# The first block of x in two transfers of 4 KB pieces, four neighbouring tokens to a partition

## Chip, cores and metric
One core of one Trainium2 chip runs the whole program. The metric is the device time of the program in microseconds (us).

## What is computed
All data are fp32; x has 2048 tokens of 512 features. Each token is normalised, goes through an attention over its own 32 heads (no token looks at another) and through a gated feed-forward layer, and the two results are multiplied and added to x. Nothing couples two tokens, so the tokens may be dealt out to partitions in any order, if the result is put back in the same order.

```python
xn = (x - mean(x)) / sqrt(var(x) + 1e-5)                       # per token
q = xn @ Wq + bq; k = repeat(xn @ Wk + bk, 4); v = repeat(xn @ Wv + bv, 4)
scores = einsum('bsdh,bseh->bsde', q, k) / 4                   # 16 x 16 per token
s = einsum('bsde,bseh->bsdh', softmax(scores), v)
nx = xn * rsqrt(mean(xn**2) + 1e-5) * ln_w
f = (silu(nx @ gate_w.T) * (nx @ up_w.T)) @ down_w.T           # 512 -> 1792 -> 512
out = x + s * silu(f)
```

## The kernel before
The 2048 tokens are four blocks of 512, and a block is four tiles of 128 tokens, one token to a partition. Blocks are worked on in pairs. The eight tiles of a pair lie in the buffer xz; x_in[j] is the semaphore of tile j's arrival. Every fp32 matrix is split into a high and a low part, and each product on PE is three matmuls (high by high, low by high, high by low). The gate and up products of the two blocks of a pair are formed with seven block products in place of eight. The hidden size 1792 is 14 groups of 128 (NI), so there are 28 groups over the two pairs.

Each engine runs a list of instructions that is written out by hand, with semaphores between engines. All transfers are issued by SP (SyncE), in the order of its program: first the four tiles of block 0 (line 402, through line 310), then the norm weights (403), the first gate and up weights (337, 342), the weights of the query, key and value product (407 to 410), tiles 4 to 6 (411), the biases, tile 7, the down weights and the next gate and up weights.

The start of the program, up to the first products, is a chain of small steps:

- DVE, for tiles 0 and 1 and then for tiles 2 and 3: the statistics of each tile (`stats_tile`, line 1097, which waits for x_in), their aggregation (1074) and two variances in one instruction (1078).
- POOL: z_scale, the reciprocal root of two variances (477).
- DVE: the four tiles normalised in place (1092), then the low parts of the first gate weights (1188), then the low parts of the transposed tiles (1141), and so on down its list.
- PE: 32 warm-up matmuls (752), then four transposes of each tile (743), then the first gate and up products (597 to 618).
- ACT: the high parts of the weights (822) and of the transposed tiles (855).

DVE's list has, at this place:

```python
for j in (0, 2):
    stats_tile(j); stats_tile(j + 1)
    aggregate(j); aggregate(j + 1)
    two_variances(j)
```

At the other end of a block, x is loaded once more for the sum with the result: `load_fin_x` (line 394) loads a whole block of 1 MB in one transfer, `finish` (1301 and 1305) forms the result of a tile on DVE, and `store` (400) writes it. For block 0 this is near the middle of the program; `load_fin_x(3)` stands behind the four stores of block 0 on SP and waits until they have landed.

The second pair of blocks is loaded into xz by the same line 310, eight transfers, and its statistics (1106, `later_stats`) wait for x_in[j] at 32, the first load and the second having added 16 each.

Of the kernel before, what the change touches and what calls it, by code (L numbers as in the profile page):

```python
# [24 lines left out]
P = 128  # L25
# [27 lines left out]
def build(nc, x, wq, bq, wk, bk, wv, bv, lnw, gate_up, down, out):  # L53
    T, E = x.shape
    K = E // P
    TB = 512
    J = TB // P
# [8 lines left out]
    GATE_BANK, UP_BANK = 1, 2  # L66
    LAST = GROUPS - 1

    x_tiles = x.rearrange("(n p) e -> n p e", p=P)
    x_blocks = x.rearrange("(b j p) e -> b p j e", j=J, p=P)  # L70
    out_tiles = out.rearrange("(n p) e -> n p e", p=P)

    w_kept = nc.dram_tensor("w_kept", [NI, P, 14 * 256], F32).ap()
    wd_kept = nc.dram_tensor("wd_kept", [NI, P, 2 * E], F32).ap()
# [3 lines left out]
    with ExitStack() as ctx:  # L78
        def sb(name, shape, dt=F32):
            return ctx.enter_context(nc.sbuf_tensor(name, shape, dt))  # L80
# [4 lines left out]
        def sem(name):  # L85
            return ctx.enter_context(nc.semaphore(name))
# [8 lines left out]
        xz = sb("xz", [P, JJ, E])  # L95
# [31 lines left out]
        fin_x = (raw_tiles[:, J:JJ, :], xz[:, 0:J, :], xz[:, J:JJ, :], raw_tiles[:, J:JJ, :])  # L127
# [17 lines left out]
        x_in = [sem(f"x_in{j}") for j in range(JJ)]  # L145
# [12 lines left out]
        fin_x_in, fin_stored = [sem(f"fin_x_in{f}") for f in range(4)], sem("fin_stored")  # L158
# [80 lines left out]
        def parts(f, j):  # L239

            return (slice(0, E // 2), slice(E // 2, E)) if f == 3 and j == J - 1 else (slice(0, E),)
# [63 lines left out]
        def _(sp):  # L305
            def load_x(pair, tiles):
                for j in tiles:
                    if pair:
                        sp.wait_ge(transposed, JJ)
                    sp.dma_start(xz[:, j, :], x_tiles[JJ * pair + j]).then_inc(x_in[j], 16)  # L310
# [85 lines left out]
            def store(f, tiles=range(J)):  # L396
                for j in tiles:
                    for n, t in enumerate(parts(f, j)):
                        sp.wait_ge(fin_done, J * f + j + n + 1)
                        sp.dma_start(out_tiles[J * f + j, :, t], fin_x[f][:, j, t]).then_inc(fin_stored, 16)  # L400

            load_x(0, range(0, J))
            sp.dma_start(lnw_sb[:], lnw).then_inc(lnw_in, 16)
            load_gate(0)
            load_up(0)
# [38 lines left out]
            for g in range(NI, GROUPS):  # L444
                load_wd(g + NI)
                if NI < g < LAST:
                    load_w(g + 1)
                if g == NI:
                    store(0)
                    load_fin_x(3)  # L450
                if g == NI + 2:
                    load_fin_x(1)
                    load_fin_x(2)
                if g - NI - 2 in FINISH_IN:
                    store(1, (FINISH_IN.index(g - NI - 2),))
            for u in range(ITEMS - NI, LATE):
                load_wd(u)
            for u in range(LATE, ITEMS):
                load_late_wd(u)
            store(2)  # L460
            store(3)
            sp.wait_ge(fin_stored, 16 * (J * 4 + 1))
# [608 lines left out]
        def _(dve):  # L1071
# [21 lines left out]
                                  ALU.subtract, ALU.mult).then_inc(z_done, 1)  # L1093

            def stats_tile(j):
                dve.wait_ge(x_in[j], 16)
                dve.bn_stats(stats[:, j, :], xz[:, j, :]).then_inc(bn_done, 1)  # L1097

            def x_variance(first):
# [2 lines left out]

            def later_stats(tiles):
                for j in tiles:
                    dve.wait_ge(x_in[j], 32)
                    dve.bn_stats(stats[:, j, :], xz[:, j, :]).then_inc(bn_done, 1)

            def later_variance():
# [206 lines left out]
            for j in (0, 2):  # L1315
                stats_tile(j)
                stats_tile(j + 1)
                aggregate(j)
                aggregate(j + 1)
                two_variances(j)  # L1320
# [7 lines left out]
            for j in range(J, JJ):  # L1328
                stats_tile(j)
                aggregate(j)  # L1330
                variance(j)
                mean_of(j)
                if j == J:
                    lo_qkv(0)
                    lo_qkv(1)
# [25 lines left out]
            for g in range(1, NI):  # L1361
                if g > 1:
                    c12(g - 1)
                attention(shares[g][0])
                if g > 1:
                    times_up1(g - 1)
                sums(g + 1)
                lo_a(g + 1)
                if g == 1:
                    t_lo(0, 3)  # L1370
                if g == 4:
                    later_stats(range(0, J))
                if g == 5:
                    later_stats(range(J, JJ))
                if g == 6:
                    later_variance()
                if g == 7:
                    norms_out()
                if g - 1 in SPREAD_IN:
                    transpose_spread(SPREAD_IN.index(g - 1))  # L1380
                attention(shares[g][1])
                c22(g)
                lo_s(g + 1)
                if g == NI - 1:
                    z2_lo_part(0)
                    z2_lo_part(1)
                attention(shares[g][2])
                times_up0(g)
                attention(shares[g][3])
# [76 lines left out]
```

## Time and profile before

| | |
|---|---|
| median of 3 runs | 473.5 us (473.32 to 473.61) |
| profiled execution, its own time | 473.5 us |
| its span in the profile | 471.7 us, so 1.8 us lie around the span |
| PE busy | 464.5 us, 98% of the span |
| DVE, ACT, POOL busy | 412.3, 243.8, 121.0 us |
| moved by DMA | 105.70 MB, mean 224 GB/s |

The span is the time from the first to the last recorded instruction. A time in the rows is in us from the start of the span, a mean duration in ns. SPq is SP's queue of DMA issues: its durations are those of the issue, not of the transfer; "DMA to landing" is the time from an issue's start until its data has arrived.

### The profile page before, as it was taken

To read this page: it belongs to the slowest core of one execution; us is meant where nothing else is said; L and a number is where in the kernel's file an instruction comes from. 1 tells how busy PE (TensorE), PEld (TensorE's weight loads), DVE (VectorE), ACT (ScalarE), POOL (GpSimd) and SP (SyncE) were. 2 spreads that over 40 slices of the span, in tenths; PEclk is the share of its full clock that TensorE was granted. 3 is DMA by queue.
4 is the path that set the end of the run, shared out by engine and by line. 5 is a ranking of instruction groups with operands and counts; after the bars stand their busy time and mean duration, and the time that the engine had idled before them with its cause. 6 is when DMAs were issued, how large, how long until landed. Compare 5 with 4: busy or idle time off the path is not lost.

```text
span 471.7 us, 6230 instructions
## 1 busy us (share of the span) xinstructions
PE 464.5 (98%) x2130; PEld 390.7 (83%) x2130; DVE 412.3 (87%) x559; ACT 243.8 (52%) x417; POOL 121.0 (26%) x104
## 2 busy tenths in 40 slices
PE   6999999999999999999999999999999999999997
PEld 6999888888888888888888888888888888888886
DVE  6999778987898898889979898999999888888994
ACT  4785566568588888554112545225325335358102
POOL 2931213116222112233353111000011111127920
PEclk9999999999999999999999999999999999999999
DMA  8606997579789986564374659545656655514762
GB/s 279 245 1 247 336 390 264 222 265 270 194 255 306 304 362 255 179 259 137 131 248 152 225 189 367 194 195 214 222 201 223 224 200 201 200 46 134 287 248 89
DMA packets 44623, 105.70 MB, mean 224 GB/s; under 512 B 20272, under 2 KB 21808, under 8 KB 41264
## 3 DMA queue, kind: packets, MB, share of 16 engines
q1 hardware_dynamic: 44592, 105.31, 63.2%
q8 instruction: 17, 0.28, 0.2%
q14 instruction: 14, 0.11, 0.1%
HBM read 69.90 MB, written 35.40 MB: 223 GB/s over the span
## 4 chain that ended last, share of the span: by engine, by line
PE 95%; DVE 3%; DMA 1%; POOL 0%; issue 0%; SPq 0%; ACT 0%; DVEq 0%; POOLq 0%
PE gu_ps L561 18%; PE gu_ps L559 18%; PE gu_ps L562 18%; PE y_ps L701 8%; PE y_ps L702 8%; PE y_ps L703 8%; PE gu_ps L703 3%; PE gu_ps L701 3%; PE gu_ps L702 3%; PE gu_ps L729 2%; PE gu_ps L730 2%; PE gu_ps L734 2%; DMA xz<-x 1%; DVE stats L1097 1%; DVE w_ops L1188 1%; DVE z_lo L1141 1%
## 5 line engine op out<-in xcount | busy, mean ns | idle before, releaser
L562 PE MATMUL gu_ps<-z_hi,w_ops 128*128 128x512 f32 x378 | 147.1, 389 | 0.0
L561 PE MATMUL gu_ps<-z_lo,w_ops 128*128 128x512 f32 x378 | 147.1, 389 | 0.0
L559 PE MATMUL gu_ps<-z_hi,w_ops 128*128 128x512 f32 x378 | 147.0, 389 | 0.0
L501 POOL TENSOR_TENSOR h_lo<-h,h_hi 128x512 fp32r<-128x512 f32 x28 | 37.0, 1322 | 229.3 <-ACT h_hi L931 229.2
L559 PEld LDWEIGHTS gu_ps<-z_hi,w_ops 128*128 128x128 f32 x378 | 71.0, 188 | 14.9
L562 PEld LDWEIGHTS gu_ps<-z_hi,w_ops 128*128 128x128 f32 x378 | 70.9, 188 | 14.7
L561 PEld LDWEIGHTS gu_ps<-z_lo,w_ops 128*128 128x128 f32 x378 | 71.0, 188 | 14.6
L701 PE MATMUL y_ps<-wd_ops,h_hi 128*128 128x512 f32 x168 | 65.6, 390 | 0.0
L703 PE MATMUL y_ps<-wd_ops,h_lo 128*128 128x512 f32 x168 | 65.5, 390 | 0.0
L702 PE MATMUL y_ps<-wd_ops,h_hi 128*128 128x512 f32 x168 | 65.5, 390 | 0.0
L931 ACT ACTIVATE h_hi<-h 128x512 fp32r<-128x512 f32 x28 | 17.6, 630 | 58.9 <-DVE h L1230 58.9
L1272 DVE TENSOR_TENSOR prod<-scores,qkv 128x1024 f32<-128x1024 f32 x32 | 43.2, 1352 | 0.8
L1254 DVE TENSOR_TENSOR prod<-qkv 128x1024 f32<-128x1024 f32 x32 | 41.8, 1306 | 0.6
L1275 DVE TENSOR_REDUCE attn<-prod 128x64 f32<-128x1024 f32 x32 | 38.9, 1217 | 0.8
L1257 DVE TENSOR_REDUCE scores<-prod 128x128 f32<-128x1024 f32 x32 | 38.9, 1216 | 0.6
L701 PEld LDWEIGHTS y_ps<-wd_ops,h_hi 128*128 128x128 f32 x168 | 31.5, 188 | 6.9 <-POOL h_lo L501 0.6
L703 PEld LDWEIGHTS y_ps<-wd_ops,h_lo 128*128 128x128 f32 x168 | 31.5, 188 | 6.6
L702 PEld LDWEIGHTS y_ps<-wd_ops,h_hi 128*128 128x128 f32 x168 | 31.5, 188 | 6.4
L906 ACT ACTIVATE u<-gu_ps 128x512 f32<-128x512 f32 x27 | 16.1, 597 | 38.9 <-PE gu_ps L562 38.9
L1242 DVE TENSOR_TENSOR h_kept<-u 128x512 f32<-128x512 f32 x27 | 22.4, 828 | 12.8 <-ACT u L919 10.0
L507 POOL TENSOR_TENSOR wd_ops<-raw,wd_ops 128x512 fp32r<-128x512 f32 x14 | 19.1, 1364 | 54.8 <-ACT wd_ops L843 25.0
L501 POOL TENSOR_TENSOR h_lo<-h_kept,h_hi 128x512 fp32r<-128x512 f32 x15 | 23.4, 1558 | 35.4 <-ACT h_hi L931 34.4
(143 smaller groups left out, 748.6 us busy)
## 6 DMA issues: line engine op xcount, KB each, us to landing
w_kept<-w_ops SPq DMA_DIRECT2D x13, 1792.0 KB, 6.4
w_ops<-w_kept SPq DMA_DIRECT2D x13, 1792.0 KB, 7.4
wd_ops<-wd_kept SPq DMA_DIRECT2D x35, 512.0 KB, 4.0
raw<-gate_up SPq DMA_DIRECT2D x30, 256.0 KB, 3.7
wd_kept<-wd_ops SPq DMA_DIRECT2D x14, 512.0 KB, 7.5
xz<-x SPq DMA_DIRECT2D x16, 256.0 KB, 5.6
raw<-down SPq DMA_DIRECT2D x14, 256.0 KB, 7.8
w_ops<-wd_kept SPq DMA_DIRECT2D x7, 512.0 KB, 6.9
```

What stands on the lines that cost most here:

```text
L501: pool.tensor_tensor(lo, src, hi.bitcast(F32), ALU.subtract).then_inc(h_lo_done, 1)
L559: pe.matmul(acc, w_h, z_hi[:, zi, c, :], start=start and c == 0, stop=False, skip_group_check=True)
L561: pe.matmul(acc, w_h, z_lo[:, zi, c, :], start=False, stop=False, skip_group_check=True)
L562: end = pe.matmul(acc, w_l, z_hi[:, zi, c, :], start=False, stop=c == 1, skip_group_check=True)
L701: pe.matmul(acc, hi, wd[:, 0, t], start=n == 0, stop=False, skip_group_check=part)
L702: pe.matmul(acc, hi, wd[:, 1, t], start=False, stop=False, skip_group_check=part)
L703: pe.matmul(acc, lo, wd[:, 0, t], start=False, stop=n == NI - 1, skip_group_check=part)\
L1242: dve.tensor_tensor(h_kept[:, g % NI, :], u2[:], up, ALU.mult).then_inc(h1_done, 1)
L1254: return dve.tensor_tensor(pr, q[:, d:d + HALF, :].unsqueeze(2).to_broadcast([P, HALF, D, HKV]), k.unsqueeze(1).to_broadcast([P, HALF, D, ...
L1257: return dve.tensor_reduce(s[:, d:d + HALF, :], pr, X, ALU.add)
L1272: return dve.tensor_tensor(pr, e[:, d:d + HALF, :].unsqueeze(2).to_broadcast([P, HALF, HKV, D]), v.unsqueeze(1).to_broadcast([P, HALF, HKV ...
L1275: return dve.tensor_reduce(o[:, d:d + HALF, :], pr, X, ALU.add)
```

## The change
Block 0 is read with another view of x: partition p holds the tokens 4p to 4p+3, tile j the tokens 4p+j. The four loads of one tile (128 pieces of 2 KB each) become two loads of two tiles, 128 pieces of 4 KB each. Both tiles of a load wait on one semaphore, x_in[0] or x_in[2]. The second load of block 0's x (`load_fin_x(0)`) uses the same view, 128 pieces of 8 KB in place of 512 of 2 KB, and the four stores of block 0 write rows of 2 KB that stand 8 KB apart in memory, where they were neighbours before. In the second pair x_in[1] and x_in[3] are awaited at 16, since the first load no longer adds to them. All other blocks are read and written as before.

```diff
+    x_first = x[0:TB].rearrange("(p j) e -> p j e", j=J)
+    x_blocks = [x_first] + [x[b * TB:(b + 1) * TB].rearrange("(j p) e -> p j e", p=P) for b in range(1, T // TB)]
+    out_tiles = [out[0:TB].rearrange("(p j) e -> j p e", j=J)[j] for j in range(J)]\
+        + [out[n * P:(n + 1) * P] for n in range(J, T // P)]
-    x_blocks = x.rearrange("(b j p) e -> b p j e", j=J, p=P)
-    out_tiles = out.rearrange("(n p) e -> n p e", p=P)
...
-                        sp.dma_start(out_tiles[J * f + j, :, t], fin_x[f][:, j, t]).then_inc(fin_stored, 16)
-
-            load_x(0, range(0, J))
+                        sp.dma_start(out_tiles[J * f + j][:, t], fin_x[f][:, j, t]).then_inc(fin_stored, 16)
+
+            for j in (0, 2):
+                sp.dma_start(xz[:, j:j + 2, :], x_first[:, j:j + 2, :]).then_inc(x_in[j], 16)
...
-                dve.wait_ge(x_in[j], 16)
+                dve.wait_ge(x_in[j - j % 2 if j < J else j], 16)
...
-                    dve.wait_ge(x_in[j], 32)
+                    dve.wait_ge(x_in[j], 16 if j in (1, 3) else 32)
```

No instruction changes its place on any engine. SP's queue has two issues less at the start of its list. Before (xz is the buffer of the tiles, raw takes the gate and up weights, h_kept here the query weights):

```order
L310 DMA xz<-x 128x512 x4
L403 DMA lnw_sb<-lnw 128x4
L337 DMA raw<-gate_up 128x512
L342 DMA raw<-gate_up 128x512
L407 DMA h_kept<-wq 128x2x512 x2
```

and with the change, whose lines stand three or four further on:

```order
L406 DMA xz<-x 128x1024 x2
L407 DMA lnw_sb<-lnw 128x4
L340 DMA raw<-gate_up 128x512
L345 DMA raw<-gate_up 128x512
L411 DMA h_kept<-wq 128x2x512 x2
```

Everything behind the x loads thus stands two issues nearer to the front. On DVE, at the start of its list, the statistics of a pair of tiles had a wait each:

```order
L1097 BN_STATS stats<-xz 128x6 [waits x_in0]
L1097 BN_STATS stats<-xz 128x6 [waits x_in1]
L1074 BN_AGGR mean_var<-stats 128x2 [waits bn_done] x2
L1078 TENSOR_SCALAR z_var<-mean_var 128x2 [waits stats_done]
L1097 BN_STATS stats<-xz 128x6 [waits x_in2]
L1097 BN_STATS stats<-xz 128x6 [waits x_in3]
```

and with the change each pair has one:

```order
L1102 BN_STATS stats<-xz 128x6 [waits x_in0] x2
L1078 BN_AGGR mean_var<-stats 128x2 [waits bn_done] x2
L1082 TENSOR_SCALAR z_var<-mean_var 128x2 [waits stats_done]
L1102 BN_STATS stats<-xz 128x6 [waits x_in2] x2
L1078 BN_AGGR mean_var<-stats 128x2 [waits bn_done] x2
```

So the statistics of tile 0 now wait for tile 1 too, and those of tile 2 for tile 3.

## Rows read from the trace of the kernel before

**Rows 1.** The page, busy time by engine (us, share of the span, instructions).

```profile
PE 464.5 (98%) x2130; PEld 390.7 (83%) x2130; DVE 412.3 (87%) x559; ACT 243.8 (52%) x417; POOL 121.0 (26%) x104
```

**Rows 2.** Every wait of PE (total us, times, longest).

```profile
PE y_ps L743 <- DVE xz L1092: 1.8, 1, 1.8
PE y_ps L752 <- POOL ident L470: 1.5, 1, 1.5
PE gu_ps L597 <- ACT z_hi L855: 0.2, 1, 0.2
PE gu_ps L729 <- DVE qkv L1214: 0.2, 1, 0.2
```

**Rows 3.** Chain that ended last, 0 to 30 us (start, us, what).

```profile
1.63 4.32 DMA xz<-x
5.96 0.02 issue
5.98 0.69 DVE stats L1097
6.68 0.69 DVE stats L1097
...
8.01 0.88 POOL z_scale L477
8.89 0.03 issue
8.91 1.00 DVE xz L1092 x2
9.92 1.05 DVE w_ops L1188 x4
```

**Rows 4.** Timeline of the start (start us, us, engine line op xcount, idle before).

```profile
0.74 1.80 SPq L310 DMA_DIRECT2D xz<-x  x4
...
3.52 1.40 DVE L1097 BATCH_NORM_STATS2 stats<-xz 128x6 f32<-128x512 f32 x2 [2.66 <-DMA xz<-x]
...
5.98 1.40 DVE L1097 BATCH_NORM_STATS2 stats<-xz 128x6 f32<-128x512 f32 x2 [0.56 <-DMA xz<-x]
...
7.40 1.28 ACT L822 ACTIVATE w_ops<-raw,lnw_sb 128x128 fp32r<-128x128 f32 x4 [5.17 <-DMA raw<-gate_up]
...
7.78 2.14 DVE L1092 TENSOR_SCALAR xz<-xz,mean_var,z_scale 128x512 f32<-128x512 f32 x4
```

**Rows 5.** Line 310, issue at 2.1 us alone, tile 3 (ns min/median/max; landing).

```profile
L310 SPq DMA_DIRECT2D xz<-x x1: 432/432/432, 2.1 to 2.1; - x1
DMA to landing us min/median/max: 4.6/4.6/4.6
```

**Rows 6.** Line 377, 205 to 240 us: lone transfers of 512 KB, 4 KB pieces.

```profile
L377 SPq DMA_DIRECT2D wd_ops<-wd_kept x9: 319/319/320, 205.6 to 238.0; - x9
DMA to landing us min/median/max: 3.1/3.2/4.5
```

**Rows 7.** Line 394 at 262 us: 1 MB of x, 2 KB pieces.

```profile
L394 SPq DMA_DIRECT2D raw<-x x1: 391/391/391, 262.3 to 262.3; - x1
DMA to landing us min/median/max: 5.3/5.3/5.3
```

**Rows 8.** Stretches: stretch, length, busy (x), PEclk, DMA share, GB/s; start.

```profile
1.50:2.50 1.00, 0.98 (x5) 0.98 (x6) 0.00 (x0) 0.72 (x2) 0.00 (x0) 1.00 0.66 119
2.50:3.50 1.00, 1.00 (x6) 1.00 (x5) 0.00 (x0) 0.00 (x0) 0.00 (x0) 1.00 1.26 367
3.50:4.50 1.00, 1.00 (x7) 1.00 (x7) 0.97 (x2) 0.00 (x0) 0.00 (x0) 1.00 0.83 299
4.50:5.50 1.00, 1.00 (x12) 1.00 (x10) 0.81 (x4) 0.00 (x0) 0.00 (x0) 1.00 0.99 313
```

**Rows 9.** The same where queued 512 KB transfers of 4 KB pieces run (L381).

```profile
445.00:446.00 1.00, 1.00 (x6) 0.81 (x6) 0.97 (x2) 0.00 (x0) 1.00 (x1) 1.00 1.01 406
446.00:447.00 1.00, 1.00 (x6) 0.84 (x5) 1.00 (x2) 0.00 (x0) 1.00 (x2) 1.00 1.03 422
```

**Rows 10.** Timeline, SP and DVE at the end of block 0.

```profile
238.38 0.38 SPq L394 DMA_DIRECT2D raw<-x  x1
...
254.67 1.60 DVE L1305 TENSOR_TENSOR raw<-raw 128x512 f32<-128x512 f32 x1
...
256.29 4.32 SPq L400 DMA_DIRECT2D out<-raw  x4
262.30 0.39 SPq L394 DMA_DIRECT2D raw<-x  x1
262.73 0.50 SPq L377 DMA_DIRECT2D wd_ops<-wd_kept  x1
268.25 0.32 SPq L369 DMA_DIRECT2D w_ops<-w_kept  x1
```

## Prediction
> **What bounds the kernel now.** I read the busy times first [rows 1]: PE is busy for 464.5 of 471.7 us. What a change elsewhere can win or lose is therefore in PE's few idle places, and the waits of PE list them [rows 2]: 1.5 us before the warm-up, 1.8 us before the first transposes of x (L743), and twice 0.2 us. No wait of PE in the whole execution ends with a transfer; the rest of the idle time is the tail behind PE's last product. The change touches block 0's loads, and so the 1.8 us: PE waits there for the first normalised tiles.
>
> What sets their time stands in the chain that ended last [rows 3]. The third tile of x lands at 5.96 us, DVE takes the statistics of tiles 2 and 3 (0.69 us each), then come aggregation and variance, POOL's z_scale (0.88), and from 8.91 us DVE's list without a gap. Every 0.1 us by which this second pair of statistics starts earlier or later goes through to the end, since DVE and then PE have no slack behind it. The timeline of the start [rows 4] gives both waits of DVE: the first pair starts at 3.52 us, the second at 5.98, after 0.56 us of idling for x. Tile 3, issued at 2.11 us (0.74 and three steps of about 0.46), lands 4.6 us later [rows 5], at about 6.68: just when DVE comes to it. **So two landings are critical at once: tile 2 at 5.96 and tile 3 at 6.68.** What counts is the start of the second pair of statistics, S = 5.98.
>
> **The change, part by part.**
>
> *First pair.* Tile 0 landed in time for 3.52 us; now both tiles must be there. A lone 512 KB transfer in 4 KB pieces takes 3.1 to 4.5 us from issue to landing, median 3.2 [rows 6]. Issued at 0.74 it lands at 3.94 (3.84 to 5.24). DVE starts at 3.96, 0.44 us later than before. From the start of one pair of statistics to the next instruction behind its variance are 7.78 - 5.98 = 1.80 us [rows 4]. DVE is therefore free for the second pair at 3.96 + 1.80 = 5.76, still 0.22 us before S. The later start costs nothing as long as the second landing is not before that, and 0.22 us is also the most that can be won.
>
> *Second pair.* Issued at 1.18 us in place of 1.63 and 2.11. Its landing is not in the trace, so I bound it. From below: right behind the first pair, 0.524 MB at the 406 to 422 GB/s at which 4 KB pieces stream late in the program [rows 9] take 1.25 to 1.3 us, landing at 5.2. At the 367 GB/s of the best us of the start [rows 8] it is 5.37. Either way DVE's 5.76 decides. From above: the same megabyte has the same last byte as before, tile 3's 6.68; the start is slower than the rest of the program, with 119 GB/s in the first us of transfers and 299 and 313 in the third and fourth [rows 8], and whatever held those back may hold back pieces of 4 KB too. Between the ends lies the nearest like row: 1 MB of x in one transfer, with nothing before it, lands after 5.3 us [rows 7], from 0.74 at 6.04. It is of 2 KB pieces, so 4 KB pieces should not be later; but it runs in mid-program, without the slow first us of the start. I let these two cancel and take **6.04**. DVE then starts at 6.06, and S moves by +0.08 us. The ends for the range are 5.76 (-0.22) and 6.70 (+0.72).
>
> Here a size rule can be weighed. The rows speak for larger pieces: 406 to 422 GB/s in 4 KB pieces against 367 at best in 2 KB pieces at the start [rows 8, 9], though the two stretches differ in more than the size. The Trainium skill speaks against a gain: "DMA: Bandwidth & Descriptors", section "Specifications", puts the smallest transfer for line rate at 512 bytes, so that 2 KB pieces would already have it; by that the megabyte takes as long as before, which is the upper end, +0.72 us. No run here shows 512-byte pieces at line rate.
>
> *Statistics pair against single tiles.* Before, tile 3 could land 0.7 us after tile 2 without cost. Now tile 2 waits for tile 3. That is why "the same last byte" would mean a loss of 0.72 us and not zero: to break even, the last byte of block 0 has to come 0.7 us earlier than it did. It is the hidden price of the change.
>
> *SP's queue.* Two issues of 0.43 us and their gaps go [rows 4, 5], so all that is issued behind comes up to 0.94 us sooner. Its consumers on the chain do not wait for it in the trace, and its bytes still stand behind block 0's, so I count nothing. If these loads came later and not sooner, the first to feel it would be the gate weights that ACT takes up at 7.40 us, when they land [rows 4].
>
> *Block 0's second load and stores.* The load is issued at 238.38 and its data first used at 254.67 [rows 10], over 16 us later; pieces of 8 KB can only shorten it: nothing. The four stores are issued by 260.6 and the next load waits for them until 262.30. If scattered rows made them slower by 5 us, that load and the one of 262.73 would slip to about 268, where SP waits anyway for PE's progress before its load of 268.25, and PE waits for no transfer [rows 2, 10]. Bounds: zero to zero, with a remainder in the slower chance. The statistics of the second pair of blocks get the same wait under another number: zero.
>
> *Sum.* The profiled execution took 473.5 us, 471.7 of span and 1.8 around it, and that is also the median of the runs. 473.5 + 0.08 = **473.6 us**. A measurement of this kernel can tell about 0.2%, 0.95 us, from no change; that is more than either end of the main case.
>
> **The rivals.**
>
> - *Forecast, second pair lands between about 5.8 and 6.3 us:* S within -0.2 to +0.35, 473.3 to 473.9. Chance 0.47.
> - *The bytes take as long as before* (the size earns nothing): S = 6.70, +0.72, 474.2 us. For it: tile 3 landed at 6.68 although 1 MB at 367 GB/s takes only 2.9 us. Against it: lone transfers and [rows 7, 9]. For landings from 6.3 to 6.9, chance 0.29.
> - *The full gain:* the second pair lands by 5.76, S is set by DVE, -0.22, 473.3 us. For it: the stream rates. Against it: the first us of the start. It merges with the forecast's lower side. Chance 0.10.
> - *Slower, through the memory's side:* the pieces of one transfer lay side by side in memory; now they stand 8 KB apart, in the same 4 KB half of each 8 KB. If that halves the rate at which x comes, the megabyte after the first us takes 0.93 MB at half of 367, 5.1 us in place of 2.5. The second pair then lands at about 6.04 + 2.5 = 8.6 us, and the time is +2.6, 476.1 us. It decides (over 0.2%) once the second landing is past 6.9 us. No row shows such a pattern alone, so I can't exclude it; the spread stores and loads of the program show no stall on PE. Together with the next, chance 0.10.
> - *Slower, through PE's clock:* PE's pause before L743 ends later. The granted clock is 1.00 (2.4 GHz) there, but the count of warm-up matmuls per us doubles only after 3 us of work, from 5 to 7 up to 12 [rows 8]. Should a longer pause bring the slow pace back for those 3 us, half of it, 1.5 us, is lost: 475.1 us. Against it: the pause grows by under 0.1 us in my forecast, 0.7 at the upper end.
> - *Faster by over 0.95 us:* even both landings at once cannot give it, as DVE's own steps allow 0.22. It would need something that I do not see. Chance 0.04.
>
> **How the numbers follow.** Within 0.2% are the first three cases, 0.86. Slower by over 0.2% are the two slow mechanisms, 0.10. Faster 0.04. The predicted time is the likeliest case's, 473.6. The range takes in the full gain less 0.15 for the spread of the runs (473.15, rounded to 473.1) and the case of unchanged bytes with the same spread above (474.35, rounded to 474.3); outside are mainly the slow mechanisms, and a little below.
>
> **What would show it.** In the new profile, DVE's first statistics should start near 3.96 us and not 3.52, and its second pair between 5.8 and 6.3; the chain of waits should name the second x transfer ahead of it. PE's wait for L743 should be 1.6 to 2.1 us, the rest of PE's waits as before, and the span within 0.3 us. A second start at 6.7 says that pieces of 4 KB earned nothing. At 5.76, with DVE not idle before it, the full gain is there. I am wrong if the second start is past 6.9 us, if PE shows a new wait, or if the transposes run at half pace.

## The result and the profile after

The change takes 473.94 us (median of 22 runs, 473.81 to 474.77) against 473.49 us (22 runs beside it, 472.86 to 474.36): 1.0014 times the time, 95% interval 1.0009 to 1.002. That is 0.45 us more, within the 0.2% that I had called no change, and clear of zero. The profiled execution has a span of 472.3 us, where before it was 471.7.

The timeline of its start, which answers to [rows 4] (start us, us, engine, line, operation; in brackets the idle time before):

```profile
0.74 0.85 SPq L406 DMA_DIRECT2D xz<-x  x2
...
4.92 1.29 DVE L1102 BATCH_NORM_STATS2 stats<-xz 128x6 f32<-128x512 f32 x2 [4.05 <-DMA xz<-x]
...
6.61 1.28 DVE L1102 BATCH_NORM_STATS2 stats<-xz 128x6 f32<-128x512 f32 x2
...
7.35 1.28 ACT L826 ACTIVATE w_ops<-raw,lnw_sb 128x128 fp32r<-128x128 f32 x4 [5.12 <-DMA raw<-gate_up]
...
8.29 2.14 DVE L1096 TENSOR_SCALAR xz<-xz,mean_var,z_scale 128x512 f32<-128x512 f32 x4
...
8.88 2.25 PE L747 MATMUL y_ps<-ident,xz 128*128 128x128 f32 x16 [0.79 <-DVE xz L1096]
```

The first statistics start at 4.92 us, 1.40 later than before. The second start at 6.61 with no idle time in front of them: they no longer wait for x at all, but for DVE itself, which is free 1.69 us after it began the first pair. The normalisation begins at 8.29 against 7.78, 0.51 us late, and PE's first transposes start at 8.88, behind a pause of 0.79. Before, they started at 8.37:

```profile
8.37 2.26 PE L743 MATMUL y_ps<-ident,xz 128*128 128x128 f32 x16 [1.78 <-DVE xz L1092]
```

The landings of the two transfers, the first alone and both together (line 406, the last line of each answer; before: [rows 5]):

```profile
L406 SPq DMA_DIRECT2D xz<-x x1: 379/379/379, 0.7 to 0.7; - x1
DMA to landing us min/median/max: 4.2/4.2/4.2
...
L406 SPq DMA_DIRECT2D xz<-x x2: 379/398/416, 0.7 to 1.2; - x2
DMA to landing us min/median/max: 4.2/4.5/4.9
```

So the first pair lands at 0.74 + 4.2 = 4.9 us and the second, issued at 1.18, at 6.1.

Four stretches of the start, columns as in [rows 8]:

```profile
1.50:2.50 1.00, 0.97 (x5) 0.98 (x6) 0.00 (x0) 0.72 (x2) 0.00 (x0) 1.00 0.63 123
2.50:3.50 1.00, 1.00 (x7) 1.00 (x5) 0.00 (x0) 0.00 (x0) 0.00 (x0) 1.00 0.99 254
3.50:4.50 1.00, 1.00 (x6) 1.00 (x6) 0.00 (x0) 0.00 (x0) 0.00 (x0) 1.00 0.94 348
4.50:5.50 1.00, 1.00 (x7) 1.00 (x6) 0.58 (x1) 0.00 (x0) 0.00 (x0) 1.00 1.01 362
```

The difference is in the second stretch: 254 GB/s where there were 367, and yet the DMA engines are busy all the time (share 0.99). The pieces take longer; nobody waits to send them. The median packet of 4 KB that began in this stretch took 205 ns in this trace, and 159 ns in the trace of the kernel with the pieces side by side (below). The third and fourth stretch are faster than before, and by 5.5 us both kernels have moved 1.09 to 1.10 MB in all. The second pair lands at 6.1, where tile 3 landed at 6.68 in the profile before; in the run of the wait alone (below), whose four transfers are those of before, tile 3 landed near 6.0. So one cannot say that the change brings the last byte sooner.

PE has the same four waits as before [rows 2], and none is new:

```profile
PE y_ps L756 <- POOL ident L474: 1.5, 1, 1.5
PE y_ps L747 <- DVE xz L1096: 0.8, 1, 0.8
PE gu_ps L601 <- ACT z_hi L859: 0.2, 1, 0.2
PE gu_ps L733 <- DVE qkv L1219: 0.2, 1, 0.2
```

The wait for the transposes is shorter than before, 0.8 us in place of 1.8, though the transposes come later. PE's 32 warm-up matmuls took 6.57 us in this execution and 5.07 before. What counts is the start of the transposes, not this wait: I had named a wait of 1.6 to 2.1 us as a sign, and it is none, since the end of the warm-up moves too.

### The profile page after: what moved, and what is told of

The parts are those of the page before. It is cut to its first block, busy times and chain, and to the rows that moved or that the text cites. A ratio compares the mean times of both kernels' runs of the same rounds, so it can differ in the third digit from the quotient of the medians.

```text
span 472.3 us, 6228 instructions
## 1 busy us (share of the span) xinstructions
PE 466.0 (99%) x2130; PEld 392.2 (83%) x2130; DVE 411.8 (87%) x559; ACT 243.8 (52%) x417; POOL 120.9 (26%) x104
## 4 chain that ended last, share of the span: by engine, by line
PE 95%; DVE 4%; DMA 1%; POOL 0%; issue 0%; ACT 0%; DVEq 0%; POOLq 0%
PE gu_ps L566 18%; PE gu_ps L565 18%; PE gu_ps L563 18%; PE y_ps L705 8%; PE y_ps L707 8%; PE y_ps L706 8%; PE gu_ps L707 3%; PE gu_ps L706 3%; PE gu_ps L705 3%; PE gu_ps L733 2%; PE gu_ps L734 2%; PE gu_ps L738 2%; DVE stats L1102 1%; DMA xz<-x 1%; DVE w_ops L1193 1%; DVE z_lo L1146 1%
```

## The experiments

My theory after the result: the four-neighbour deal makes the pieces of one transfer stand 8 KB apart, and that slows them ("pitch"). Rivals: pieces of 4 KB are slow when the program starts ("size"), a transfer of 512 KB is ("one transfer"), or the common wait of two tiles is the loss.

**Four transfers with the new deal.** The view of the change, the loads and waits of before.

```diff
-            for j in (0, 2):
-                sp.dma_start(xz[:, j:j + 2, :], x_first[:, j:j + 2, :]).then_inc(x_in[j], 16)
+            for j in range(J):
+                sp.dma_start(xz[:, j, :], x_first[:, j, :]).then_inc(x_in[j], 16)
...
-                dve.wait_ge(x_in[j - j % 2 if j < J else j], 16)
+                dve.wait_ge(x_in[j], 16)
```

> The changed kernel's view of x (four neighbours to a partition) but four transfers of one tile in 2 KB pieces that stand 8 KB apart, each tile with its own wait. Theory 'size' (pieces of 4 KB are slow in the first microseconds, after showed 254 GB/s in its second one): tile 0 lands at 3.5 us and tile 1 at 4.2 as before, second statistics at 6.0, time as before within 0.1 us. Theory 'pattern' (the 8 KB pitch between a transfer's pieces is slow): tile 0 after 4.2 us, first statistics 0.7 us late or more, time +0.4 us or more.

474.35 us, ratio 1.0017 (1.0008 to 1.0027). Its second stretch, and its first statistics:

```profile
2.50:3.50 1.00, 1.00 (x7) 1.00 (x6) 0.00 (x0) 0.00 (x0) 0.00 (x0) 1.00 0.92 227
...
4.10 0.69 DVE L1102 BATCH_NORM_STATS2 stats<-xz 128x6 f32<-128x512 f32 x1 [3.24 <-DMA xz<-x]
5.11 0.69 DVE L1102 BATCH_NORM_STATS2 stats<-xz 128x6 f32<-128x512 f32 x1 [0.31 <-DMA xz<-x]
6.21 0.69 DVE L1102 BATCH_NORM_STATS2 stats<-xz 128x6 f32<-128x512 f32 x1
7.19 0.69 DVE L1102 BATCH_NORM_STATS2 stats<-xz 128x6 f32<-128x512 f32 x1 [0.29 <-DMA xz<-x]
```

Pieces of 2 KB and no common wait, and the start is as slow as in the change: 227 GB/s, tile 0 at 4.1 us and not 3.5, tile 1 at 5.1 and not 4.2, the transposes at 8.88. The size theory falls. (Tile 0 came a little before the 4.2 us that I had set for the pitch theory; the loss in time is as it said.)

**Two transfers with the old order.**

```diff
-            load_x(0, range(0, J))
+            for j in (0, 2):
+                sp.dma_start(xz[:, j:j + 2, :], x_blocks[0][:, j:j + 2, :]).then_inc(x_in[j], 16)
```

The waits are those of the change.

> Tokens in the old order, two transfers of two tiles in 2 KB pieces, one wait for a pair. Theory 'size': the first pair lands at 4.0 to 4.2 us and not at 4.9; what is left is the price of the common wait, second pair at 6.1 to 6.7, time +0.1 to +0.6 us. Theory 'one transfer' (a transfer of 512 KB is slow at the start, whatever its pieces): first pair at 4.9 us, second statistics at 6.6, time +0.5 us as the changed kernel.

473.50 us, ratio 1.0009 (0.9998 to 1.002). Stretches, first statistics and transposes:

```profile
2.50:3.50 1.00, 1.00 (x7) 1.00 (x6) 0.00 (x0) 0.00 (x0) 0.00 (x0) 1.00 1.04 404
3.50:4.50 1.00, 1.00 (x6) 1.00 (x6) 0.53 (x1) 0.00 (x0) 0.00 (x0) 1.00 1.06 401
...
3.97 1.29 DVE L1098 BATCH_NORM_STATS2 stats<-xz 128x6 f32<-128x512 f32 x2 [3.11 <-DMA xz<-x]
...
7.95 1.69 PE L744 MATMUL y_ps<-ident,xz 128*128 128x128 f32 x11 [1.07 <-DVE xz L1093]
```

With 2 KB pieces in the old order the first pair lands 3.2 us after its issue, at the 3.94 us that I had predicted for the change. "One transfer" falls too. The second lands by 5.5. The transposes start at 7.95, 0.42 us before the kernel before, and the span is 471.3.

**Two neighbours to a partition.** Pieces of 4 KB as in the change, but those of one transfer lie side by side in memory.

```diff
-    x_first = x[0:TB].rearrange("(p j) e -> p j e", j=J)
+    x_first = x[0:TB].rearrange("(h p j) e -> p h j e", h=2, j=2)
...
-                sp.dma_start(xz[:, j:j + 2, :], x_first[:, j:j + 2, :]).then_inc(x_in[j], 16)
+                sp.dma_start(xz[:, j:j + 2, :], x_first[:, j // 2, :, :]).then_inc(x_in[j], 16)
```

Block 0's second load and its stores follow the same view.

> Two neighbouring tokens to a partition: two transfers of 4 KB pieces that lie side by side in memory. Theory 'size': the first pair lands at 4.9 us as in the changed kernel, GB/s near 254 from 2.5 to 3.5 us, time +0.5 us. Theory 'pattern': it lands at 3.9 to 4.2 us, second statistics between 5.8 and 6.1, time within 0.15 us of before.

473.27 us, ratio 1.0 (0.9991 to 1.0009).

```profile
L407 SPq DMA_DIRECT2D xz<-x x1: 382/382/382, 0.7 to 0.7; - x1
DMA to landing us min/median/max: 3.3/3.3/3.3
...
2.50:3.50 1.00, 1.00 (x7) 1.00 (x5) 0.00 (x0) 0.00 (x0) 0.00 (x0) 1.00 0.97 365
...
4.11 1.28 DVE L1103 BATCH_NORM_STATS2 stats<-xz 128x6 f32<-128x512 f32 x2 [3.24 <-DMA xz<-x]
...
8.07 1.58 PE L748 MATMUL y_ps<-ident,xz 128*128 128x128 f32 x10
```

Same size, count and waits as the change; only which tokens a piece holds is another. The first pair lands 0.9 us sooner (3.3 against 4.2) and the transposes start 0.8 us sooner. Other executions bear this out: the first pair landed after 3.3 us in both other profiles with the pieces side by side, and after 4.0 and 3.9 us in both other profiles of the change's start.

**The common wait alone,** with the four transfers of before.

```diff
             def stats_tile(j):
+                if j < J and j % 2 == 0:
+                    dve.wait_ge(x_in[j + 1], 16)
                 dve.wait_ge(x_in[j], 16)
```

> The kernel before with its four transfers; only the statistics of tile 0 wait for tile 1 too and those of tile 2 for tile 3. First statistics at 4.2 us. If tile 3 lands at 6.68 again, the second start at 6.70, less 0.12 us for the statistics of a pair without a wait between (1.29 against 1.40 us): time +0.6 us. If the common wait were free, time +0.0.

473.74 us, ratio 1.0004 (0.9995 to 1.0013).

```profile
4.06 1.29 DVE L1099 BATCH_NORM_STATS2 stats<-xz 128x6 f32<-128x512 f32 x2 [3.20 <-DMA xz<-x]
...
6.04 1.29 DVE L1099 BATCH_NORM_STATS2 stats<-xz 128x6 f32<-128x512 f32 x2 [0.20 <-DMA xz<-x]
```

Tile 3 landed near 6.0 us in this execution and not at 6.68, so the second pair starts 0.06 us later than before. A pair of statistics takes 1.29 us and not 1.40, though each still has a wait of its own: both tiles are there, and the second instruction starts 0.61 us after the first. Before, tiles 1 and 3 landed only at 4.20 and 6.66 us, and their statistics started 0.02 us behind that, 0.70 us after the first of the pair; the 0.11 us were a wait for x. The expected +0.6 did not come: the landing on which I had built it varies from one execution to the next. What the common wait costs is not told apart from zero.

**A small transfer ahead.** Is it only the first large transfer that is slow? The norm weights (2 KB) are issued before x, else the change.

> The changed kernel, with the 2 KB transfer of the norm weights issued before the two of x. Theory 'pitch' (pieces of one transfer 8 KB apart are slow): x is issued 0.45 us later and still takes 4.2 us for its first pair, first statistics near 5.3 us, time 0.4 us above the changed kernel. Theory 'cold start' (the first large transfer of a program pays once, and a small one ahead of it would take that over): the first pair takes 3.2 to 3.5 us from its issue, first statistics at 4.5 to 4.7, time 0.2 us or more below the changed kernel.

474.55 us, ratio 1.0031 (1.0021 to 1.0042).

```profile
5.53 1.29 DVE L1102 BATCH_NORM_STATS2 stats<-xz 128x6 f32<-128x512 f32 x2 [4.67 <-DMA xz<-x]
```

The first pair, issued at 1.18, took 4.3 us; the small transfer took nothing over. "Cold start", in this form, falls.

**The pattern late in the program.** In the change, two of the later loads of x are cut in halves: that of block 0 (pieces 8 KB apart) and that of block 3 (2 KB pieces, side by side).

> The changed kernel, with two of the later loads of x split in halves of 512 KB: block 0's near 239 us in 4 KB pieces 8 KB apart, block 3's near 263 us in 2 KB pieces that lie side by side. Their data are used many us later, so the time stays that of the changed kernel. Theory 'pitch': the halves near 239 us land 0.5 us or more later after their issue than a lone 512 KB load of contiguous pieces (3.1 to 3.6 us; 3.2 median). Theory 'pitch only when cold': the first half lands in 3.1 to 3.6 us, as the half near 263 us does.

One execution, 473.77 us. The pair of issues near 239 us, the pair near 263, and the first of the latter alone:

```profile
L399 SPq DMA_DIRECT2D raw<-x x2: 377/404/432, 238.6 to 239.1; - x2
DMA to landing us min/median/max: 5.3/5.7/6.1
...
L399 SPq DMA_DIRECT2D raw<-x x2: 390/430/471, 262.8 to 263.2; - x2
DMA to landing us min/median/max: 3.4/3.8/4.3
...
L399 SPq DMA_DIRECT2D raw<-x x1: 390/390/390, 262.8 to 262.8; - x1
DMA to landing us min/median/max: 3.4/3.4/3.4
```

The comparison isn't clean, since a 512 KB weight load is issued just ahead of the first pair. The same megabyte behind the same weight load took 5.9 us before, in 2 KB pieces, and 5.7 in the change, in 8 KB pieces without gaps. In halves 8 KB apart the last byte came 6.1 us after an issue that was itself 0.47 us later, 6.5 in all: 0.6 to 0.8 us more. In this one execution, then, the pattern seems to cost something in mid-program too, in the size of the 0.9 us at the start.

**The deal without gaps.** Block 0 in one transfer, 128 pieces of 8 KB, all statistics behind it.

```diff
-            for j in (0, 2):
-                sp.dma_start(xz[:, j:j + 2, :], x_first[:, j:j + 2, :]).then_inc(x_in[j], 16)
+            sp.dma_start(xz[:, 0:J, :], x_first).then_inc(x_in[0], 16)
```

> The deal of the changed kernel, but block 0 comes in one transfer of 1 MB, 128 pieces of 8 KB without gaps between them. All statistics wait for it. Theory 'pitch': the deal itself costs nothing, the megabyte streams at 365 GB/s or more from the second microsecond and lands 4.5 to 5.3 us after its issue, at 5.2 to 6.0, as in the runs with contiguous pieces; second statistics 1.69 us behind the landing, at 6.9 to 7.7, time +0.8 to +1.6 us over the kernel before, all of it from the common wait. Theory 'large pieces are slow when cold': landing at 6.1 us or later.

474.71 us, ratio 1.0034 (1.0021 to 1.0048).

```profile
DMA to landing us min/median/max: 4.9/4.9/4.9
...
5.67 1.29 DVE L1101 BATCH_NORM_STATS2 stats<-xz 128x6 f32<-128x512 f32 x2 [4.81 <-DMA xz<-x]
```

The same deal of tokens, read without gaps: the whole megabyte is there at 5.64 us, 0.5 us before the change has it in two transfers. (From 2.5 to 3.5 us it ran at 303 GB/s and then at 401; I had expected 365 at once.) It is the placement of the pieces within a transfer that costs, not the deal; and waiting for the whole megabyte loses more than it saves.

**Tiles 2 and 3 together.** An attempt at a better kernel, in the old order: tiles 0 and 1 alone, 2 and 3 in one transfer.

> Tokens in the old order; tiles 0 and 1 in a transfer each as before, tiles 2 and 3 together in one of 512 KB (2 KB pieces, one wait). First statistics at 3.5 us as before; DVE is free for the second pair at 5.3. If the second pair lands at 5.5 us as in the run with two plain transfers, the second start is 5.5 and the transposes start at 7.8 us, 0.5 us before the kernel before: time -0.3 to -0.5 us against it. If the slow third and fourth microsecond of the kernel before comes back, it lands at 6.0 to 6.7: time -0.1 to +0.5 us.

474.35 us, ratio 1.0026 (1.0017 to 1.0036), the fastest of 11 runs at 473.76.

```profile
3.39 1.30 DVE L1098 BATCH_NORM_STATS2 stats<-xz 128x6 f32<-128x512 f32 x2 [2.53 <-DMA xz<-x]
...
6.96 1.29 DVE L1098 BATCH_NORM_STATS2 stats<-xz 128x6 f32<-128x512 f32 x2 [1.77 <-DMA xz<-x]
...
3.50:4.50 1.00, 1.00 (x6) 1.00 (x6) 1.00 (x2) 0.00 (x0) 0.00 (x0) 1.00 0.71 225
```

A miss: the second pair lands at 6.9 us. The stream fell to 225 GB/s from 3.5 to 4.5 us, as it had in the kernel before (299), while the run with two transfers had kept 401.

**One and three.** Does the stream pause where the third transfer begins? Tile 0 alone, tiles 1 to 3 in the second transfer, old order.

> Tokens in the old order, 2 KB pieces; tile 0 in a transfer of its own, tiles 1 to 3 together in the second, so that block 0 takes two transfers. Theory 'third transfer' (the stream pauses where the third transfer of the program begins; it did after 512 KB in the kernel before and with tiles 0, 1 and 2-3, and only after the whole megabyte with two transfers): no pause within block 0, the second transfer lands 4.2 to 4.6 us after its issue at 1.18, at 5.4 to 5.8, and the GB/s from 3.5 to 4.5 us are 370 or more. Theory 'fixed time or bytes' (a pause near 3.5 us or after 512 KB, however the transfers are cut): it lands at 6.2 us or later, GB/s from 3.5 to 4.5 us under 300. In both, tile 1 waits for the megabyte, so the time is 0.5 to 1.5 us above the kernel before.

474.81 us, ratio 1.0033 (1.0019 to 1.0047).

```profile
2.50:3.50 1.00, 1.00 (x7) 1.00 (x6) 0.14 (x1) 0.00 (x0) 0.00 (x0) 1.00 0.80 186
3.50:4.50 1.00, 1.00 (x7) 1.00 (x7) 0.55 (x1) 0.00 (x0) 0.00 (x0) 1.00 0.99 365
```

The second transfer landed 5.0 us after its issue, at 6.2, which is the lower edge of what "fixed time or bytes" asks. From 3.5 to 4.5 us the rate is near what "third transfer" asks, but a pause came all the same, a microsecond earlier and within the second transfer. Neither theory holds as I put it. Why the stream of the first megabyte pauses, and when, stays open.

**Once more side by side, with the change beside it.** The kernel with two neighbours to a partition and the change, unaltered, on one chip.

> The kernel with two neighbours to a partition once more, beside the change and the kernel before on one chip. By the placement of the pieces as the cause, it is 0.4 to 0.9 us faster than the change and within 0.3 us of the kernel before.

> The changed kernel once more, on the same chip as the three above: 0.3 to 0.8 us above the kernel before, first statistics between 4.7 and 5.1 us.

Side by side 473.37 us (12 runs), the change 473.96 (11 runs, ratio 1.0012, 1.0003 to 1.0021), the kernel before 473.42 (30 runs). By the medians the placement is worth 0.6 us, and ten of the twelve side-by-side runs are below the fastest of the change (473.87). The ratio of the side-by-side kernel to the one before is 1.0005 (0.9995 to 1.0015). In the change's profile the first statistics start at 4.73 us and the rate from 2.5 to 3.5 us is 258 GB/s; side by side it is 426:

```profile
4.73 1.29 DVE L1102 BATCH_NORM_STATS2 stats<-xz 128x6 f32<-128x512 f32 x2 [3.86 <-DMA xz<-x]
2.50:3.50 1.00, 1.00 (x7) 1.00 (x6) 0.00 (x0) 0.00 (x0) 0.00 (x0) 1.00 1.02 258
...
4.04 1.28 DVE L1103 BATCH_NORM_STATS2 stats<-xz 128x6 f32<-128x512 f32 x2 [3.18 <-DMA xz<-x]
2.50:3.50 1.00, 1.00 (x7) 1.00 (x6) 0.00 (x0) 0.00 (x0) 0.00 (x0) 1.00 1.06 426
```

The slow second microsecond is no accident of one execution.

**Fewer warm-up matmuls,** 24 and not 32, else side by side.

> As the run before, with 24 warm-up matmuls and not 32. In the profile with 32 they ended at 8.00 us, 0.07 us before the first transposes. If they bound the start in part of the executions, the median falls by 0.05 to 0.2 us; if DVE and the gate weights bind it (ACT took them at 7.60 us), it stays within 0.1 us. If the pace of PE needs the last eight, the transposes run at half pace and the time is 1 us or more higher.

473.89 us (11 runs), ratio 1.001 (1.0001 to 1.0018); its transposes start at 8.05 us, with 32 at 8.07 and 8.02. The pace of the transposes is the full one, 273 ns each. The warm-up does not bind the start. But the higher median is no accident: the 11 runs fall into two groups. Four have a mean granted clock of 0.999 or 1.0 and take 473.22 to 473.40 us; seven have 0.996 and take 473.86 to 474.15. With 32 warm-up matmuls only one of 23 side-by-side runs has a clock under 0.998 (0.995, the last point of this document). Leaving out eight matmuls thus went with a lower clock in most runs, and those took about 0.6 us longer. The profiled run is one of the four without it, so where in the program the clock was lower is not shown.

No version beats the kernel before by more than the measurement can tell. The kernels with two transfers without gaps and 32 warm-up matmuls are level with it.

## Why the prediction was right, and where it was not

- *The place.* All that moved is the start of the transposes, as forecast: 8.88 - 8.37 = 0.51 us, against 0.6 in the span and 0.45 in the medians. The other profiles bear out that a shift there goes through to the end: two plain transfers, transposes at 7.95 us, span 471.3; side by side, 8.07 and 471.5; the common wait alone, 8.33 and 471.7; four transfers dealt, 8.88 and 472.3. No new wait of PE, and nothing from the stores, the second load or SP's queue.
- *The second pair's landing:* forecast 6.04, measured 6.1, and of no effect. That it fits is luck: I had let two unknown differences cancel and had not counted the gaps. Without gaps the second pair landed at 5.5 us, in 2 KB and in 4 KB pieces.
- *The first pair's landing is the term that was mis-sized:* forecast 3.94 us from lone transfers of contiguous 4 KB pieces [rows 6], measured 4.9, within the upper end of 5.24 that I had kept, but well off the value I took. I had placed the danger of the 8 KB gaps in a rival of its own and left the main case with the price of a contiguous transfer. By that mistake the forecast was 473.6 us (+0.08) and the result 473.94 (+0.45).
- *What bounds the second statistics:* I had DVE free 1.80 us after the first start and x as the last to come. The 1.80 was read from a pair whose second tile came late: 0.11 us of it was waiting for tile 3. With both tiles there it is 1.69 us, and with the first start at 4.92 DVE is the bound: 4.92 + 1.69 = 6.61. The same 0.11 us is why a start 0.63 us late costs only 0.51; by my own 1.80 the sum would have been 6.72, +0.74 us. So two errors partly made up for each other. The 0.11 us is also why 0.22 us was not the most that could be won.
- *The signs.* Three that I had named did not come: first statistics near 3.96 (4.92), second between 5.8 and 6.3 (6.61, where I had put the case of unchanged bytes), and a wait of PE of 1.6 to 2.1 us (0.8). The span moved by 0.6 and not by 0.3 at most. The time, 473.94 us, lies just above what I gave the forecast itself (473.3 to 473.9) and within the range, because the range reached up to a case with another mechanism; that is luck too.
- *The rivals.* "The bytes take as long as before" is not shown either way: the second pair landed at 6.1 us (6.0 and 6.3 in two other profiles), tile 3 before at 6.68 in one profile and near 6.0 in the run of the wait alone. "Slower through the memory's side" named the right cause, the pieces 8 KB apart, with far too high a price: the rate fell from 365 to 254 GB/s for one microsecond, not to half for the whole megabyte. It cost 0.8 us against the same pieces side by side, and the merging gave 0.3 us of that back in the profiles. (In the other executions the transposes start at 8.69 and 8.64 us in the change and at 8.02 side by side.) The full gain was there to be had: without gaps the transposes start 0.30 to 0.42 us sooner than before in the profiles, though it doesn't show in the medians.
- *The hidden price of the common wait* was argued from one landing at 6.68 us. With the landing as it came in the run of the wait alone, it is nil.
- *The size rule.* The Trainium skill ("DMA: Bandwidth & Descriptors", section "Specifications") has 512 bytes as the smallest transfer for line rate, so that 4 KB should give nothing over 2 KB. The runs agree: 404 and 401 GB/s in 2 KB pieces, 365 and 385 in 4 KB pieces, both without gaps. But I had drawn from it that the megabyte would take as long as before, and it did not: two transfers had it there at 5.5 us in 2 KB pieces (old order) as well as in 4 KB pieces side by side, against 6.0 to 6.7 with four, so in these profiles the merging and not the size of the pieces brought the last byte forward.
- *The pitch.* The same page of the Trainium skill, section "Latency and other measured facts", lists slow copies within HBM where the rows of a tile stand 512 KiB or more apart, and infers, unverified, that the partitions' streams meet on the same memory channels. Here, in loads of x, 8 KB from piece to piece is enough for a loss, a figure far below that table. Whether the reason is the same, no run here shows.

## What to carry to other kernels

When several small loads are merged, keep the pieces of each transfer side by side in memory: a deal that gives each partition longer runs but leaves gaps within a transfer cost 0.6 us here and the length earned nothing that could be measured, while dealing fewer neighbours per transfer gives the same length without gaps. Only the distance of 8 KB was tried; whether other distances cost as much is open. Price a transfer at the start of a program by a transfer of the same pattern, and keep the term for the first landing apart from that for the last, since a common wait can shift the bound to the engine that comes behind it. Read how long an engine takes from a place where its inputs are there, or its waits are counted as its work. A forecast that rests on one landing in one profile is uncertain by the spread of that landing, here 0.6 us.

## What the runs showed that I had not expected

- The same megabyte of x, 128 pieces of 4 KB in each of two transfers, came at 254 and 258 GB/s in its second microsecond with pieces 8 KB apart and at 365 and 426 with pieces side by side; in 2 KB pieces, with two or four transfers, at 227 with gaps and at 367 to 404 without.
- The pace of the warm-up matmuls doubles at a time that differs between executions, from 4.5 us in the kernel before to after 7.5 us in the change, while the granted clock reads 1.00 throughout. The 3 us that I had read for this hold for one execution only. No start of the transposes depended on it in these profiles.
- In some executions PE's granted clock falls to the lower level (1.2 GHz) soon after the start. The profile of the second side-by-side run caught one, at 475.84 us against its median of 473.37. Its stretches (columns as before):

```profile
8.00:11.00 3.00, 2.23 (x16) 1.68 (x16) 1.60 (x4) 1.49 (x5) 0.52 (x1) 1.00 1.08 372
11.00:14.00 3.00, 2.03 (x9) 1.76 (x10) 3.00 (x9) 3.00 (x9) 1.88 (x3) 0.73 1.06 356
14.00:17.00 3.00, 3.00 (x12) 2.47 (x12) 2.97 (x7) 2.97 (x6) 2.92 (x4) 0.71 0.73 252
17.00:20.00 3.00, 3.00 (x17) 2.62 (x16) 2.90 (x9) 1.25 (x3) 2.59 (x4) 1.00 1.03 396
```

  The granted clock averages 0.73 and 0.71 in two stretches and is 1.00 around them. Before it fell, PE had waited 0.9 us for its transposes and 1.6 us for ACT, whose gate weights landed at 9.5 us and not at 7.6. The profiles of the one-transfer kernel and of the one-and-three kernel, both with a late start of the transposes, show the same dip. Other profiles with as long a pause before the transposes (1.9 us with the four dealt transfers, 2.1 us with tiles 2 and 3 together) do not show it. So the rival by which a longer pause brings the lower clock back exists, but only in some executions. It has no part in the change's result: none of its 33 runs has a mean granted clock under 0.998.
